# Gate scores with the rows as stationary operand, and other orders of work at attention's chunk changes

## What is computed

```python
x = x + 0.5 * _L0_ffn_ref(_layernorm(x, axis=-1), ...)
x = x + _L0_attn_ref(_layernorm(x, axis=-1), ...)
x = x + 0.5 * _L0_ffn_ref(_layernorm(x, axis=-1), ...)
...
scores = xf @ gate_w.T + gate_b + bias          # 8 experts
top_scores, top_idx = jax.lax.top_k(scores, TOP_K)   # 2 of them
h = jax.nn.silu(jnp.einsum('td,ehd->teh', xf, w1) + b1)
y = jnp.einsum('teh,edh->ted', h, w2) + b2
```

## Time and profile before

| what | value |
|---|---|
| three runs, us | 839.11, 839.63, 842.44; median 839.63 |
| the profiled execution, us | 840.33 |
| its span, first to last instruction | 838.6 |
| mean granted TensorE clock | 0.961 |
| TensorE busy | 765.6 us, 91% |
| VectorE busy | 608.2 us, 73% |
| ScalarE busy | 360.8 us, 43% |
| GpSimd busy | 233.6 us, 28% |

### The profile page before, as it was taken

One profiled execution on the slowest core, in us unless ns is written; L12 is line 12 of the kernel. 1 busy time (PEld: TensorE's weight loads), 2 busy tenths in 40 slices (PEclk: granted clock), 3 DMA queues, 4 the chain that ended last, 5 costly groups with the idle time before them and its releaser, 6 DMA issues.

```text
span 838.6 us, 14107 instructions
## 1 busy us (share of the span) xinstructions
PE 765.6 (91%) x4218; PEld 423.7 (51%) x4219; DVE 608.2 (73%) x1024; ACT 360.8 (43%) x626; POOL 233.6 (28%) x225
## 2 busy tenths in 40 slices
PE   8688899999996998998999999999924999999998
PEld 5336455656563444444444444445513666666663
DVE  6885756666656569999989998896876555555557
ACT  5855333343433436445544654443260333333331
POOL 3212644445532001101211111102102444444432
PEclk9899999999997998899899999999976999999999
DMA  9974648974744701610352121265472573333698
GB/s 315 392 292 138 234 142 318 338 290 160 255 146 108 180 1 51 100 51 1 78 99 26 52 26 14 63 229 127 170 277 91 206 268 120 113 117 121 221 311 307
DMA packets 44955, 137.27 MB, mean 164 GB/s; under 512 B 5488, under 2 KB 5488, under 8 KB 41584
## 3 DMA queue, kind: packets, MB, share of 16 engines
q1 hardware_dynamic: 27536, 86.38, 28.7%
q0 software_dynamic: 17376, 50.34, 21.8%
HBM read 85.32 MB, written 51.38 MB: 163 GB/s over the span
## 4 chain that ended last, share of the span: by engine, by line
PE 77%; DVE 12%; ACT 3%; DMA 3%; issue 2%; POOL 2%; SPq 0%; DVEq 0%; ACTq 0%; POOLq 0%
PE bank L653 62%; PE bank L647 5%; PE bank L746 3%; DMA space<-xn_rows,slot_src 2%; PE bank L916 2%; PE bank L696 1%; PE bank L832 1%; DVE space L1406 1%; DVE space L1685 1%; POOL space L574 1%; DMA space<-x_in 1%; PE bank L850 1%; DVE space L1682 1%; DVE bst L1397 1%; ACT space L1147 1%
## 5 line engine op out<-in xcount | busy, mean ns | idle before, releaser
L653 PE MATMUL bank<-space 128*128 (+3 forms) x2958 | 580.5, 349 | 22.4 <-DVE space L1470 12.8
L653 PEld LDWEIGHTS bank<-space 128*128 128x128 f16 (+1 forms) x2958 | 276.3, 99 | 270.7 <-issue 25.4
L578 POOL DMA_INDIRECT y_rows<-space,slot_dst x78 | 89.2, 1144 | 158.3 <-DVE space L1538 157.7
L574 POOL DMA_INDIRECT space<-xn_rows,slot_src x78 | 81.7, 1047 | 121.7 <-PE bank L647 62.3
L1094 ACT ACTIVATE space<-bank 128x512 f16<-128x512 f32 x78 | 46.5, 597 | 145.3 <-PE bank L647 137.0
L1538 DVE TENSOR_SCALAR space<-bank,slot_gate 128x512 f32<-128x512 f32 x78 | 58.5, 750 | 60.3 <-PE bank L653 59.3
L1525 DVE SCALAR_TENSOR_TENSOR space<-bank,space 128x352 f32<-128x352 f32 x78 | 40.8, 523 | 59.3 <-PE bank L653 42.0
L1104 ACT ACTIVATE space<-bank 128x384 f16<-128x384 f32 x78 | 38.2, 489 | 94.5 <-PE bank L746 94.5
L647 PE MATMUL bank<-ident,space 128*128 128x128 f32 x440 | 66.5, 281 | 12.5 <-DMA space<-xn_rows,slot_src 10.6
L1519 DVE TENSOR_TENSOR space<-bank,space 128x512 f16<-128x512 f32 x78 | 53.9, 690 | 32.2 <-ACT space L1094 30.8
L1682 DVE SCALAR_TENSOR_TENSOR space<-space,cang 128x512 f32<-128x512 f32 x84 | 63.0, 750 | 5.5 <-ACT space L1186 3.3
(11 more groups left out here) (199 smaller groups left out, 747.3 us busy)
## 6 DMA issues: line engine op xcount, KB each, us to landing
space<-ffn_w SPq DMA_DIRECT2D x8, 1472.0 KB, 10.2
w_saved<-space SPq DMA_DIRECT2D x8, 1472.0 KB
space<-w_saved SPq DMA_DIRECT2D x8, 1472.0 KB, 9.1
xn_rows<-space SPq DMA_DIRECT2D x8, 1024.0 KB, 6.5
space<-y_rows SPq DMA_DIRECT2D x16, 512.0 KB, 6.5
space<-x_in SPq DMA_DIRECT2D x7, 1024.0 KB, 11.8
space<-att_w SPq DMA_DIRECT2D x12, 518.0 KB
space<-y_rows POOLq DMA_DIRECT2D x6, 1024.0 KB, 9.1
```

The lines of the kernel that those rows point to most:

```text
L574: gp.indirect_dma_start(dst, None, rows, bass.IndirectOffsetOnAxis(ap=index, axis=0)).then_inc(done, 16)
L578: gp.indirect_dma_start(y_rows, bass.IndirectOffsetOnAxis(ap=slot_dst[:, t:t + 1], axis=0), yo[:, t % 2], None).then_inc(y_st[t % 2], 16)
L653: last = pe.matmul(dst, a, b, start=(n == 0), stop=(n == len(terms) - 1))
```

## The change

Scores: the transposed rows become the stationary operand (128 by 128) and the gate's 8 columns move; 4 products for each row tile, whose result already lies as 128 tokens by 8. `copy_raws`, `score_back`, their buffers and semaphores go, and `s_gate` counts tiles instead of pairs. First chunk: `normalise(0, 2)` is moved ahead of `x_high(0, 1)`, and the second offset ahead of `first_low(0)`. Chunk changes: on TensorE `spread` is moved behind `leave_low(c+1, 2)` and `mean_square` behind `leave_low(c+1, 3)`; on ScalarE `squares` stands behind two `x_low`, and `gate_high` behind all of them; in units 0, 3 and 6 `evacuate(u+2, 3)` is moved ahead of `trig(u+1)`, and in 3 and 6 both normalisations too; on VectorE the offset stands right behind `gate_low` in units 3 and 6. `HEAD_START` is 4.

```diff
-HEAD_START = 5
+HEAD_START = 4
...
             def score(ph, q):
-                pe.wait_ge(s_xtc, NT * ph + 2 * q + 4)
-                if NPAIR * ph + q:
-                    pe.wait_ge(s_rawc, NPAIR * ph + q)
-                products(bank[2][0:E, P:P + PAIR],
-                         [(gw[:, k, :], xgT[ph][:, q % 2, k, :]) for k in range(KD)]).then_inc(s_raw, 1)
-
-            def score_back(ph, q):
-                pe.wait_ge(s_rawc, NPAIR * ph + q + 1)
                 for i in (0, 1):
                     n = 2 * q + i
-                    last = pe.transpose(bank[2][:, n * E:(n + 1) * E], raws[ph][:, i * P:(i + 1) * P], ident[0:E, 0:E])
-                last.then_inc(s_gate, 1)
+                    pe.wait_ge(s_xtc, NT * ph + n + 3)
+                    products(bank[2][:, n * E:(n + 1) * E],
+                             [(xgT[ph][:, q % 2, k, i * P:(i + 1) * P], gw[:, k, :]) for k in range(KD)]).then_inc(s_gate, 1)
...
                         leave_low(c + 1, 0)
                         leave_low(c + 1, 1)
-                        spread(u + 1)
                         transpose_tile(c + 1, 3)
                         if c:
                             project_out(c - 1, 1)
                         leave_low(c + 1, 2)
+                        spread(u + 1)
+                        leave_low(c + 1, 3)
                         mean_square(u)
-                        leave_low(c + 1, 3)
                         logits(c + 1)
...
             def copy_pair(ph, q):
                 if NPAIR * ph + q >= 2:
-                    act.wait_ge(s_raw, NPAIR * ph + q - 1)
+                    act.wait_ge(s_gate, 2 * (NPAIR * ph + q - 1))
...
                 x_high(0, 0)
+                normalise(0, 2)
                 x_high(0, 1)
-                normalise(0, 2)
                 normalise(0, 3)
...
                         x_high(c + 1, 2)
-                        squares(u)
                         if c:
                             out_tile(c - 1, 0)
                         x_low(c + 1, 0)
                         x_low(c + 1, 1)
+                        squares(u)
                         x_high(c + 1, 3)
+                        x_low(c + 1, 2)
+                        x_low(c + 1, 3)
                         gate_high(u - 1)
-                        x_low(c + 1, 2)
                         mean_squares(u)
-                        x_low(c + 1, 3)
...
+                        elif p == 0 and c < NCH - 1:
+                            evacuate(u + 2, 2)
+                            repeat_roots(u)
+                            evacuate(u + 2, 3)
+                            if u == 0:
+                                trig(u + 1)
+                            normalise(c + 1, 0)
+                            normalise(c + 1, 1)
+                            if u:
+                                trig(u + 1)
+                            continue
...
-                v.wait_ge(s_gate, NPAIR * (ph + 1))
+                v.wait_ge(s_gate, NT * (ph + 1))
...
+                offset(NCH + 1, 0, c_rstd, 2, TPC)
                 first_low(0)
                 first_low(1)
-                offset(NCH + 1, 0, c_rstd, 2, TPC)
...
-                    shift = (lambda: offset(NCH + c + 2, 0, c_rstd)) if p == 0 and c < NCH - 1 else None
-                    convolve(u + 1, (lambda: gate_low(u - 1)) if u else None, shift)
+
+                    def shift():
+                        if p == 0 and c < NCH - 1:
+                            offset(NCH + c + 2, 0, c_rstd)
+
+                    def low_and_shift():
+                        gate_low(u - 1)
+                        shift()
+
+                    if u:
+                        convolve(u + 1, low_and_shift)
+                    else:
+                        convolve(u + 1, None, shift)
```

More of the change, by code:

```diff
@@ L209, in build @@
         S, S2, OH1, OH2, KEY, M8, QP = (lay([NT, E]) for _ in range(7))
-        raws_first = Layout(lay.at - 6 * NT * E)([PAIR], rows=E)
         CE, SC, EX = (lay([E, NT]) for _ in range(3))
@@ L238, in build @@
         xgT = [xgT_first, Layout(PAIRS * 4 * (CH + HALO))([2, KD, PAIR])]
-        raws = [raws_first, Layout(WEND - 2 * D)([PAIR], rows=E)]
         x2_tail = lay([TPC, D])
@@ L311, in build @@
         s_gw, s_gwc = sem("s_gw"), sem("s_gwc")
-        s_raw, s_rawc = sem("s_raw"), sem("s_rawc")
         s_gate = sem("s_gate")
@@ L492, in _ @@
             sp.dma_start(b1_bc, b1.partition_broadcast(P)).then_inc(b1_in[1], 16)
-            sp.wait_ge(s_gate, 2 * NPAIR)
+            sp.wait_ge(s_gate, 2 * NT)
             for g in range(NCH):
@@ L963, in attention @@
                         spread(u + 1)
-                        score_back(1, 0)
                         score(1, 1)
                         project_out(c - 1, 0)
-                        score_back(1, 1)
                         project_out(c - 1, 1)
@@ L991, in attention_end @@
                 mean_square(UNITS - 1)
-                score_back(1, 2)
                 score(1, 3)
@@ L998, in attention_end @@
                 spread_roots(UNITS - 1)
-                score_back(1, 3)
                 pe.wait_ge(c_norm, UNITS - 1)
@@ L1007, in attention_end @@
                 pair_in(1, 6)
-                score_back(1, 4)
                 score(1, 5)
                 pair_in(1, 7)
-                score_back(1, 5)
                 score(1, 6)
-                score_back(1, 6)
                 score(1, 7)
-                score_back(1, 7)
             heads = headmean[:, :].rearrange("p (h c) -> p h c", h=2)[:, :, 0]
@@ L1022, in _ @@
             products(bank[4][:, 0:E], [(ones[:, :], gw[:, k, :]) for k in range(KD)]).then_inc(s_gw, 1)
-            for q in range(NPAIR + 2):
+            for q in range(NPAIR + 1):
                 if q < NPAIR:
@@ L1027, in _ @@
                     pe.wait_ge(s_gwc, 1)
-                if 1 <= q <= NPAIR:
+                if q:
                     score(0, q - 1)
-                if q >= 2:
-                    score_back(0, q - 2)
             pe.wait_ge(consts, 2)
@@ L1080, in copy_pair @@
                                    bank[n % 2][:, :].rearrange("p (k c) -> p k c", k=KD), ACT.Copy).then_inc(s_xtc, 1)
-            def copy_raws(ph, q):
-                act.wait_ge(s_raw, NPAIR * ph + q + 1)
-                if NPAIR * ph + q:
-                    act.wait_ge(s_gate, NPAIR * ph + q)
-                act.activation(raws[ph], bank[2][0:E, P:P + PAIR], ACT.Copy).then_inc(s_rawc, 1)
             def slots(ph):
@@ L1291, in attention @@
                         copy_pair(1, 1)
-                        copy_raws(1, 0)
                         gate_high(u - 1)
                         out_tile(c - 1, 0)
-                        copy_raws(1, 1)
                         trig(u + 1)
@@ L1319, in attention @@
                             out_tile(c - 1, 3)
-                        if p == 0 and c < NCH - 1:
-                            normalise(c + 1, 0)
-                            normalise(c + 1, 1)
             def attention_end():
@@ L1328, in attention_end @@
                 copy_pair(1, 3)
-                copy_raws(1, 2)
                 mean_squares(u)
@@ L1332, in attention_end @@
                 repeat_roots(u)
-                copy_raws(1, 3)
                 gate_high(u)
@@ L1336, in attention_end @@
                 copy_pair(1, 5)
-                copy_raws(1, 4)
                 copy_pair(1, 6)
-                copy_raws(1, 5)
                 copy_pair(1, 7)
-                copy_raws(1, 6)
                 normalise_row(1, 0)
-                copy_raws(1, 7)
                 for n in range(1, NT):
@@ L1353, in _ @@
                     copy_pair(0, q)
-                if q:
-                    copy_raws(0, q - 1)
                 if q >= 2:
```

## The result

The changed kernel takes 859.99 us (855.42 to 861.36) where the kernel before takes 840.09 (839.11 to 842.44): ratio 1.0223, 95% interval 1.018 to 1.0267. The forecast was 835.7, in a range of 831.5 to 843. It is slower, by 1.8 to 2.7%. The larger part is the mechanism of rival A, the clock, which had a chance of 0.16; the new orders of work add the rest.

The account below looks back on a forecast made before the run. TensorE had 77% of the last-ending chain, but VectorE decided in places. Terms -1.4 + 0.1 - 0.3 + 1.7 - 1.8 - 2.2 = -3.9 took the profiled 840.33 to 836.4, or 835.7 as median; range 831.5 to 843.

Parts of the forecast that it names:

- rival A: Score stages: 8-column scores may leave TensorE at 1.2 GHz, a pair taking 5.3 us; 849 to 857, or 840; chance 0.16.
- Opening, "0 us": Opening stage: score savings stay hidden behind VectorE's work and routing still starts at 34.42; 0 us.
- the cover: Opening: VectorE's weight split ends at 34.42 and only then routing begins, leaving TensorE 0.8 us to spare.
- The page against the row: Score stages: skill page says transposes don't engage the full clock, implying 849 to 857; trace rows spoke against it.
- Score cost, 1.7 a pair: Each pair's scores: sixteen 8-column records take 1.7 us instead of 2.03; bounds 1.6 and 2.03.
- First chunk, -1.4: First chunk: earlier normalisation and offset let the logits start 1.4 us earlier; bounds 1.2 to 1.6.
- This arrives whole: First chunk: the 1.4 us gain passes on entirely, as everything to unit 0's 6.6 us wait is TensorE's.
- Chunk changes, -0.3: Units 1, 4, 7: TensorE gets ahead, idles 3 to 4 us in unit 4, and only 0.3 us is kept.
- rival B: Unit 4: TensorE's lead becomes an idle gap that costs the clock; +2 on units 5 and 6, 838; chance 0.2.
- Added waits, +1.7: Units 6 and 7: recur(7) waits 1.3 for trig(7), gate_low(6) waits 1.0, less 0.6 slack; bounds 0 and 2.9.
- Units 10 and 11 and the last pairs, -1.8 - 2.2: Units 10, 11 and pairs 4 to 7: cheaper scores and removed waits save 1.8 and 2.2 us.
- HEAD_START, 0: Kernel end: one addition moves behind VectorE's last output tile, costing 0 us; bounds -0.2 and +0.4.

Follow-up runs that it names:

- number 8: Kernel before with only the chunk-change orders (first chunk, scores and HEAD_START 5 as before): 845.03 us, ratio 1.0039.
- number 9: Kernel before with only the score part, each score record moving 64 columns instead of 8: 837.16 us, ratio 0.9963.
- number 5: Changed kernel with each score record moving 64 columns (the 8 gate columns repeated 8 times): 841.46 us, ratio 1.0011 to the kernel before.
- number 7: Changed kernel with four wide products (256 columns, result unused) once before the opening's first score: 857.77 us, ratio 1.021 to the kernel before.
- number 13: Changed kernel, scores narrow, with the score stages' row transposes made as ordinary matmuls against the identity: 855.34 us, ratio 1.0147 to the kernel before.
- number 10: Kernel before with the 64-column score part and the first chunk's edit, chunk changes and HEAD_START as before: 837.23 us, ratio 0.9956.
- number 2: Kernel before with everything of the change except the score part (all orders and HEAD_START 4): 846.40 us, ratio 1.0061.
- number 3: Changed kernel with VectorE's offset at chunk changes back behind the two angle taps: 859.23 us, ratio 1.0188 to the kernel before.
- number 12: Kernel before with HEAD_START 4 alone: 839.69 us, ratio 0.999.
- numbers 1: Kernel before with the 8-column score part alone, all orders and HEAD_START as before: 855.97 us, ratio 1.0156.

## Why the prediction was wrong, point by point

- **Opening, "0 us".** The step that failed. It took VectorE's end at 34.42 as the cover and left the clock to rival A. The cover was good for 0.5 a pair; at half clock a pair takes 5.02 instead of the 2.7 reckoned. Rival A's arithmetic held: 5.3 a pair, opening ended at 48.0, 13.6 past the cover; measured 5.02, 46.2 and 11.9. It gave 857 with the last pairs, and 860 came.
- **The weight given to rival A.** It was 0.16, on two readings. The rise ahead of 11.59 in the earlier trace rows was read as having little behind it but transposes and the start of one pair's scores. As a reading that holds: numbers 8 and 9 rise within the transposes alone. The stretch at 549.5 in the earlier trace rows had projections of 512 columns in it. But neither row said anything of a stage in which 8-column records fill 3.3 of 5.0 us of each pair, and numbers 5 and 7 show that these decide: widened, they let the clock rise; narrow, they lose it even once it is up. The trace of before had no such stage, only the mean square's few records and eight ahead of the first transposes, so this was an unmeasured resource, and it should have been bounded by both ends with about even chances.
- **The page against the row.** The prediction set the Trainium skill (TensorE: Matmul & The Clock Gate, Part 4: PE-mode transpose), by which transposes don't engage the full clock, against its rows, and sided with the rows "as far as transposes go". The traces of numbers 8 and 9 differ from the page: the clock rose at 8.65 and 8.64, within the first sixteen transposes. So siding with the rows was right, and the mistake lay in taking the rows as evidence on the narrow records too. Number 5 keeps the transposes and is cured; number 13 would fit the page but the narrow records' smaller share explains it as well.
- **Score cost, 1.7 a pair.** Right at full clock: 1.70 (617.93 to 619.63), 1.74 with 64 columns.
- **First chunk, -1.4.** Right in kind, a little small. From last scatter to recur(0), the six traces without the edit have 33.6 to 35.1, mean 34.4, the nine with it 31.9 to 33.1, mean 32.5: -1.9. "This arrives whole" is wrong for the total: number 10 is no faster than number 9, nor number 2 than number 8; in the one trace of number 10 the gain is given back where the clock fell.
- **Chunk changes, -0.3.** The account of the gap was right (409; 3 to 4). That it would be harmless was wrong in number 8, where rival B, at 0.2, came with 1.25 ahead of recur(6) and 1.1 ahead of recur(9). In the changed kernel's trace the gap was there and the clock stayed.
- **Added waits, +1.7.** Near in size by luck. trig(7)'s 1.3 exists (number 3) but is hidden behind a larger one that was overlooked, the offset ahead of the angle taps, 2.54. gate_low(6) was to wait 1.0 and waits 0.28. The diff showed the offset's move, and the earlier trace rows leaves out GpSimd; the rule to ask of each moved step what it waits for was not applied to it.
- **Units 10 and 11 and the last pairs, -1.8 - 2.2.** Right as a cost: -4.2 in number 9. In the changed kernel the clock turned it into +4.9.
- **HEAD_START, 0.** Right (number 12).

With the clock back in the score stages, the whole change is number 5, and it is no faster than before: +0.6 where -3.9 had been forecast. Of the forecast's terms, the scores' -4.0 nearly came (number 9, -3.6 in the runs), while the orders, reckoned at +0.1, cost 4.1 (number 2).

## What to carry to other kernels

A matmul with a 128x128 stationary operand and a few moving columns is cheap in TensorE's time and can cost the clock of the whole stage: a stage made only of transposes and 8-column products ran at half speed with TensorE busy all the time. Repeating the moving columns, to 64 or 128, cost 0.003 to 0.006 us a record here and brought the clock back, though not in every stage of every execution; so look, in a stage that a change rewrites, at what wide work it takes away. And a gain in front of a stage that loses the clock at times is worth its face value only once the runs have shown it. Last, one trace is one execution: where the clock rose or fell differed between traces of the same program text, so a price read behind such a place needs the runs beside it.

## What the runs showed of the hardware

- Records of a 128x128 float32 stationary operand cost 0.106 us with 8 columns, 0.109 with 64 and 0.112 with 128 at full clock; with 8 columns at half clock 0.205.
- TensorE busy 20.00 of 20 us stood at 1.2 GHz for the whole opening with scores of 8 columns (routing at 46.26, and at 46.11 and 46.06 in numbers 1 and 3); with 64 columns it rose at 10.2, 8.6 and 15.2 in three traces, with 128 at 11.6.
- TensorE's transposes do not keep the clock down by themselves: in two traces it rose at 8.64 and 8.65, within the first sixteen of them.
- At an idle gap of 3.7 us in unit 4 the clock fell inside or just behind it in seven traces and stayed full in one; in number 3 it fell behind a gap of 2.14.
- Four products of 256 columns raised the clock at 10.6; transposes and 8-column records behind them lost it at 20.9 without a gap.
- The view writes a granted clock of 1.00 ahead of the trace's first change; in the opening of the changed kernel that was wrong for 50 us.
